# Moving three norms, an hT copy and the row copies of batches 2 and 3 to ScalarE, with new step lists

## What is computed

```python
x = _layernorm(x + _L0_attn_ref(x, ...))     # 16 query heads, 4 kv heads, width 8, RMS norm, rotation,
                                             # softmax(50 tanh(s / 50)), causal
x = _layernorm(x + _L0_xattn_ref(x, ctx...)) # attention to 32 context rows, FiLM, an S4D convolution over
                                             # the sequence (in the Fourier basis), layernorm h, gelu MLP 128-512-128,
                                             # layernorm
x = _layernorm(x + _L0_ffn_ref(x, ...))      # 2 shared experts for all tokens, 8 routed ones, the top 2 per token
```

## Time and profile before

| | |
|---|---|
| runs | 546.08, 549.91, 554.17 us, median 549.91 |
| profiled execution | 546.51 us, span 544.3 us |
| PE busy | 438.0 us, 80% |
| DVE, ACT busy | 332.0 us (61%), 324.6 us (60%) |
| POOL busy | 229.3 us, 42% |
| PE clock granted, mean | 0.926 of full speed |

### The profile page before, as it was taken

One profiled execution on the slowest core, in us unless ns is written; L12 is line 12 of the kernel. 1 busy time (PEld: TensorE's weight loads), 2 busy tenths in 40 slices (PEclk: granted clock), 3 DMA queues, 4 the chain that ended last, 5 costly groups with the idle time before them and its releaser, 6 DMA issues. The chain is left out here.

```text
span 544.3 us, 9650 instructions
## 1 busy us (share of the span) xinstructions
PE 438.0 (80%) x3369; PEld 316.0 (58%) x3369; DVE 332.0 (61%) x991; ACT 324.6 (60%) x541; POOL 229.3 (42%) x296
## 2 busy tenths in 40 slices
PE   3572575577989979978889899899998799898990
PEld 2430141154747834556645677488588797698970
DVE  7989997587575576877662678266266320434224
ACT  4158987758985687967799424413355454364531
POOL 3064616523622064451522441746145677144521
PEclk9996756678989989999999999999998999999996
DMA  3798300004020000000000205203227797779831
GB/s 94 253 219 147 100 2 0 0 1 138 1 81 1 20 0 2 1 0 1 2 1 1 49 31 187 86 11 85 58 83 222 210 314 246 203 234 284 274 98 39
DMA packets 39699, 51.40 MB, mean 94 GB/s; under 512 B 8802, under 2 KB 28804, under 8 KB 39652
## 3 DMA queue, kind: packets, MB, share of 16 engines
q1 hardware_dynamic: 37156, 45.65, 29.3%
q0 software_dynamic: 2496, 5.15, 2.6%
HBM read 41.12 MB, written 13.86 MB: 101 GB/s over the span
## 5 line engine op out<-in xcount | busy, mean ns | idle before, releaser
L1107 ACT ACTIVATE probs<-ring_s 128x512 f32<-128x512 f32 x160 | 84.8, 607 | 30.1 <-PE ring_s L784 21.2
L1299 POOL TENSOR_SCALAR_AFFINE_SELECT probs<-probs 128x256 f32<-128x256 f32 (+1 forms) x96 | 50.4, 557 | 103.3 <-ACT probs L1113 103.2
L1160 ACT ACTIVATE g_ring<-ring_s,w_blk 128x128 f32<-128x128 f32 x184 | 52.5, 370 | 48.8 <-PE ring_s L982 48.7
L784 PE MATMUL ring_s<-qT,kT 128*128 128x512 bf16 (+3 forms) x256 | 60.6, 336 | 24.3 <-ACT probs L1107 20.0
L1113 ACT ACTIVATE probs<-probs 128x2560 f32<-128x2560 f32 x32 | 74.6, 2344 | 1.9
L1221 POOL TENSOR_TENSOR rstd<-var_eps,neg_half 128x4 f32<-128x4 f32 x24 | 24.7, 1027 | 102.0 <-DVE var_eps L1547 101.9
L1350 POOL DMA_INDIRECT token_pairs<-y_blk,x_blk x46 | 44.5, 967 | 34.4 <-DVE y_blk L1893 26.0
L801 PE MATMUL bank_o<-probs,vv 128*32 128x128 f32 (+3 forms) x512 | 46.8, 515 | 9.7 <-POOL probs L1299 9.0
L784 PEld LDWEIGHTS ring_s<-qT,kT 128*128 128x128 bf16 x256 | 21.7, 104 | 55.5 <-ACT probs L1107 41.9
L982 PE MATMUL ring_s<-xT_blk,w_blk 128*128 128x128 f32 x368 | 50.3, 281 | 1.7 <-DMA w_blk<-expert_pack 0.9
L982 PEld LDWEIGHTS ring_s<-xT_blk,w_blk 128*128 128x128 f32 x368 | 45.6, 195 | 3.2 <-ACT g_ring L1160 1.5
(11 more groups left out here) (376 smaller groups left out, 942.3 us busy)
## 6 DMA issues: line engine op xcount, KB each, us to landing
w_blk<-expert_pack SPq DMA_DIRECT2D x46, 514.0 KB, 4.8
expert_pack<-in_L_ffn_W SPq DMA_DIRECT2D x16, 256.0 KB, 9.4
expert_rows<-blank SPq DMA_DIRECT2D x6, 520.0 KB, 3.9
x_blk<-expert_rows SPq DMA_DIRECT2D x10, 260.0 KB, 4.6
y_pair<-token_pairs SPq DMA_DIRECT2D x8, 256.0 KB, 4.0
x_in<-in_x SPq DMA_DIRECT2D x4, 256.0 KB, 3.1
cosm<-in_c_cos SPq DMA_DIRECT2D x1, 1024.0 KB, 7.4
sin_fwd<-in_c_sin_fwd SPq DMA_DIRECT2D x1, 1024.0 KB, 10.4
```

What stands on the lines that cost most here:

```text
L784: last = mm(bank[:, c:c + w], kT[:, r, p // 2, P * j:P * (j + 1)], qT[:, p, P * j:SEQ], start=True, stop=True)
L1107: f(probs[:, pair % PAIRS_HELD, SEQ * n:SEQ * (n + 1)], ring_s[k % BANKS][:, :], ACT.Tanh, scale=1.0 / (CAP * float(np.sqrt(np.float32(HD) ...
L1160: last = f(g_ring[:, s % RING, P * n:P * (n + 1)], ring_s[s % 2][:, P * n:P * (n + 1)], ACT.Gelu, bias=w_blk[:, k % SLOTS, HID + n:HID + n ...
L1299: last = g.affine_select(out=v, in_=v, compare_op=ALU.is_ge, fill=0.0, base=0, pattern=[[0, v.shape[1]], [1, P]], channel_multiplier=-1)
```

## The change

For batches 2 and 3 (`LATER = 2`), DVE no longer scales the tiles in `h`, `ff_norm` and `x2`. It copies rstd and computes -mean * rstd into a small tile `late_scale` (two instructions on 128x4), and ACT applies them with four Identity activations. ACT also takes `hT.2`, `hT.3` and `copies.2`, `copies.3`. All four step lists are written anew, from their start, not only where these steps stand.

```diff
+LATER = 2
+            def norm_late(b, n, src, dst):
+                act.wait_ge(late_scaled[b - LATER], n + 1)
+                for j in range(NT):
+                    last = f(dst[:, j, :], src[:, j, :], ACT.Identity, scale=late_scale[:, b - LATER, n, 0, j:j + 1],
+                             bias=late_scale[:, b - LATER, n, 1, j:j + 1])
+                return last
+
+            def h_step(b):
+                norm_late(b, 0, xt, fa).then_inc(h_ready, 1)
+
+            def ff_norm(b):
+                norm_late(b, 1, xt, fa).then_inc(ff_scaled, 1)
+
+            def x2_step(b):
+                norm_late(b, 2, fa, x2[:, b, :].rearrange("p (j d) -> p j d", j=NT)).then_inc(x2_ready, 1)
+
+            def hT_step(b):
+                act.wait_ge(hT_ps, b + 1)
+                act.wait_ge(up_ps, HC * b)
+                f(hT[:, :], bank_r[:, :], ACT.Copy).then_inc(hT_sb, 1)
+
+            def copy_rows(b):
+                act.wait_ge(x2_ready, b + 1)
+                act.wait_ge(rows_copied, b)
+                if b % GB == 0:
+                    act.wait_ge(scattered[b // GB - 1], 16 * 2 * NT * GB)
+                for k in range(2):
+                    last = f(x_rows[:, k, NT * (b % GB):NT * (b % GB + 1), 0:D], x2[:, b, :].rearrange("p (j d) -> p j d", j=NT), ACT.Copy)
+                last.then_inc(rows_copied, 1)
...
-                if b >= GB and b % GB == 0:
-                    pool.wait_ge(scattered[b // GB - 1], 16 * 2 * NT * GB)
...
+            def norm_later(b, n):
+                roots[0] += 1
+                dve.wait_ge(rstd_ready, roots[0])
+                scale = late_scale[:, b - LATER, n, :, :]
+                op(v.tensor_copy(scale[:, 0, :], rstd[:, :]))
+                stt(out=scale[:, 1, :], in0=mean_var[:, :, 0], scalar=-1.0, in1=rstd[:, :], op0=ALU.mult, op1=ALU.mult).then_inc(late_scaled[b - LATER], 1)
+                dve.wait_ge(late_scaled[b - LATER], n + 1)
...
             def h_step(b):
+                if b >= LATER:
+                    return norm_later(b, 0)
                 norm_end(xt, fa).then_inc(h_ready, 1)
```

(`ff_norm` and `x2_step` on DVE get the same two lines.) Of the lists, one line of DVE's and two of ACT's:

```diff
-    steps squares.0 rms.0 rope.0 parts.0 v.0 copies.0 states qT.0.1 qT.0.3 vf.0 vf.1 vf.2 qT.0.5 pack angles.0
+    steps squares.0 rms.0 rope.0 parts.0 v.0 copies.0 states qT.0.1 squares.1 qT.0.3 vf.0 vf.1 rms.1 vectors pack
...
-    ff_out.1 s.3.7.0 s.3.7.1 s.3.7.2 s.3.7.3 s.3.7.4 exp.3.7 x2T.1 gates_exp.1 blk_gelu.0 blk_gelu.1 blk_gelu.2
-    blk_gelu.3 x1T.3 blk_gelu.4 blk_gelu.5 blk_gelu.6 blk_gelu.7 cross_exp.3 attnT.3 blk_gelu.8 gelu.2.0 gelu.2.1
+    exp.3.6 s.3.7.0 s.3.7.1 s.3.7.2 s.3.7.3 s.3.7.4 exp.3.7 x2T.1 gates_exp.1 blk_gelu.0 blk_gelu.1 x1T.3 blk_gelu.2
+    blk_gelu.3 blk_gelu.4 cross_exp.3 blk_gelu.5 blk_gelu.6 h.2 attnT.3 blk_gelu.7 hT.2 gelu.2.0 gelu.2.1 gelu.2.2
```

More of the change, by code:

```diff
@@ L107 @@
[L107 to L111, removed]
@@ new lines @@
+    mask.3.0 root mask.3.1 shift.1 shape_out.1 resid.1 mask.3.2 root root mask.3.3 mask.3.4 mask.3.5 shift.2 copies.0
+    root ff_norm.1 mask.3.6 root mask.3.7 copies.1 root root shape_out.2 resid.2 root scatter.1.0 scatter.1.1
+    scatter.1.2 scatter.1.3 root ff_norm.2 root scatter.1.4 scatter.1.5 scatter.1.6 shift.3 scatter.1.7 shape_out.3
+    resid.3 root root ff_norm.3 root blk_out.16 blk_out.17 blk_out.18 blk_out.19 blk_out.20 blk_out.21 blk_out.22
+    scatter.3.0 scatter.3.1 scatter.3.2 blk_out.23 blk_out.24 blk_out.25 scatter.3.3 blk_out.26 blk_out.27 blk_out.28
@@ L201 @@
-    turns.0 vectors vf.3 products.0 amounts.0 angles.1 turns.1 angles.2 turns.2 oT.0 products.1 amounts.1 tokens.0
-    squares.1 rms.1 angles.3 turns.3 products.2 w1 oT.1 tokens.1 parts.1 oT.2 tokens.2 amounts.2 copies.1 evacuate.0
-    oT.3 tokens.3 evacuate.1 products.3 yT.0 amounts.3 evacuate.2 qT.1.1 v.1 proj.0 evacuate.3 qT.1.3 qT.1.5 x1.0
-    x_norm.0 xn.0 first_tap squares.2 rms.2 oT.4 cross.0 tokens.4 soften.0 spectra oT.5 parts.2 tokens.5 film.0.0
-    film.0.1 film.0.2 film.0.3 modulate.0 oT.6 copies.2 tokens.6 spectrum.0 v.2 oT.7 qT.2.1 qT.2.3 tokens.7 yT.1
@@ L221 @@
-    weigh.63 weigh.64 blkT.68 blkT.69 weigh.65 blkT.70 weigh.66 blkT.71 weigh.67 weigh.68 weigh.69 weigh.70 weigh.71
-    pairs.2 pairs.3 out_begin.2 settle.77 out_end.2 out_begin.3 out_end.3
+    steps squares.0 rms.0 rope.0 parts.0 v.0 copies.0 states qT.0.1 squares.1 qT.0.3 vf.0 vf.1 rms.1 vectors pack
+    angles.0 turns.0 vf.2 vf.3 qT.0.5 products.0 amounts.0 angles.1 turns.1 oT.0 angles.2 turns.2 products.1 tokens.0
+    amounts.1 oT.1 evacuate.0 angles.3 turns.3 products.2 evacuate.1 tokens.1 oT.2 tokens.2 parts.1 copies.1
@@ new lines @@
+    amounts.2 oT.3 w1 tokens.3 evacuate.2 qT.1.1 yT.0 products.3 amounts.3 qT.1.3 proj.0 evacuate.3 qT.1.5 x1.0 v.1
+    first_tap x_norm.0 squares.2 rms.2 oT.4 cross.0 tokens.4 spectra soften.0 oT.5 film.0.0 tokens.5 film.0.1
+    film.0.2 film.0.3 xn.0 modulate.0 parts.2 copies.2 oT.6 tokens.6 qT.2.1 spectrum.0 oT.7 v.2 qT.2.3 tokens.7 yT.1
+    proj.1 x1.1 shape_out.0 cross.1 h_norm.0 soften.1 h.0 squares.3 hT.0 rms.3 x_norm.1 qT.2.5 oT.8 film.1.0 film.1.1
+    tokens.8 film.1.2 film.1.3 xn.1 modulate.1 oT.9 parts.3 tokens.9 ffT.0 ff_norm.0 oT.10 copies.3 tokens.10
@@ L487, in build @@
         out_scaled = sem("out_scaled")
+        late_scaled = [sem(f"late_scaled{n}") for n in range(B - LATER)]
         pair_used = sem("pair_used")
```

181 lines of the change are left out of this document (93 added, 88 removed).

## The result

The changed kernel takes 530.19 us as the median of four runs (528.00, 530.16, 530.22 and one of 1090.26 that nothing here explains and that the comparison leaves out), beside 551.26 us of the kernel before on the same chip. The ratio is 0.961, 95% interval 0.952 to 0.971. It is faster by 3.9%, twice the 2% or so that I had forecast, and 1.2 us inside the low end of the range of 529 to 551. The profiled executions are closer to each other, 546.51 and 530.16 us, spans 544.3 and 528.3, since the one of before is quicker than all but one of its other runs.

The account below looks back on a forecast made before the run. Bound: early, no engine full, each waiting for others in order; from 163 us PE nearly full. Profiled 546.5, front -7, back -2: 537.5, plus about half of that execution's 3.4 us below the median: 539 us; range 529 to 551.

Parts of the forecast that it names:

- The front's times: Up to batch 1's first tanh: ACT's new list laid out with old durations, that tanh at 116 to 118 against 127.80 us.
- 66.1: Front, ACT's list: from 56.8 us, six tanhs, an exp and the sines of round 1 end at 66.1 us.
- 93: Front, ACT's list: after 81.9 us, ten tanhs and two exps end at 93 us.
- The term for the front: Attention 10 to 12 us earlier, S4D kernel 7; the shorter taken as reaching the end: -7 us, bounds 0 and -12.
- Behind it PE is nearly full and shifts as a whole: After the front: PE's later work moves earlier with the front's lead, no term of its own.
- Rival 3: More goes right: front gains 12 us, back 4, some of PE's 16 idle us from 163 to 299 go: 528; chance 0.13.
- The back: Where the moved steps stand: PE's small waits filled by half units, -2 us, bounds 0 and -4.
- The five gaps: Back: PE's waits of 0.69 to 0.88 us for one copy, 3.8 us in all, filled by half units.
- The floor: First expert group's rows land at about 381.7, PE takes them at 382.80: of 3.0 us only 1.1 usable.
- the half units: Back: shared expert work ahead of each use hides the moved norms, costing PE nothing; otherwise six times 0.8 us.
- Rival 1: The front's lead is not carried: front 0 to -3, back -1, 543 to 548, take 546; chance 0.24.
- Rival 2: Back: ACT stops at six norms for `late_scale`, gelus queue; 2.5 us each, 15 us, gives 554; chance 0.17.

Follow-up runs that it names:

- e_front_old: Changed kernel with the old order ahead of batch 1's first scores: 539.9 us, 9.6 more than the changed kernel rerun beside it, ratio to the kernel before 0.987.
- e_mid_only: Kernel before with the new order only from batch 1's first scores to the first shared expert unit, old engines: 554.66 us, ratio 0.979.
- e_lists_tail: Changed kernel with DVE's old order from `blkT.49`, and norms, hT and row copies back on DVE and POOL: 522.9 us, ratio to the kernel before 0.956.
- e_tail_old: Changed kernel with DVE's old order from `blkT.49` on: 526.23 us, 4.1 less than the changed kernel rerun beside it.
- f_act_pe: Kernel before with the new order of the front on ACT and PE alone: 580.33 us, ratio 1.025.
- f_dve_pool: Kernel before with the new order of the front on DVE and POOL alone: 580.36 us, ratio 1.027.
- e_lists_only: Kernel before with all four new lists, but norms, hT and row copies left on DVE and POOL: 541.3 us, ratio 0.955.
- sets 2 and 4: Two calls of follow-up runs, each on one chip with the kernel before beside them, which took 565.65 and 565.57 us.
- e_norms_back: Changed kernel with DVE's old order from `blkT.49` and the six norms back on DVE, hT and row copies on ACT: 539.03 us, ratio to the kernel before 0.952.
- sets 1 and 3: The call that measured the change and a later call of follow-up runs; the kernel before took 551.26 and 548.17 us in them.
- set 3: One call of follow-up runs on one chip, variants of the changed kernel and its rerun, beside the kernel before at 548.17 us.
- e_changed_again: The changed kernel itself, run once more: 530.33 us beside 548.17 of the kernel before, ratio 0.970.

## Why the prediction was right, and where it was not

The measured time is in the range, by 1.2 us, and that is luck: two terms that the sum does not have, -7.1 us in the middle and +5.4 at the end, nearly cancel. Without the second the time would have been some 525 us, under the range.

- **The front's times were right.** First value product 54.9 us (forecast 51 to 55), idle ahead of pair 7's tanhs 3.27 (under 5), cast 0.41 (near 0.5), last powers of round 3 end at 112.7 (112), first tanh of batch 1 at 117.46 (116 to 118). Laying the new list out by hand with the old durations worked here. Two of its sums are off: "66.1" adds up to 67.4, which the next line has right again, and "93" to 91.6, and these 1.4 us are carried to the end, where they brought the forecast closer to what was measured. The first product came 6.7 us earlier, not 8.
- **The term for the front was too small, -7 for -10.3.** I took the S4D strand, 7 us earlier, as the shorter chain. Wrong as put: the new middle takes 167.6 to 169.5 us behind new and old fronts, whether the strand's last powers end 5 us ahead of batch 1's tanh (changed) or some 7 (e_front_old), so it follows attention, and the strand has slack. The pass has the move of `xT.2` in its 116 to 118, but no price for it; it is worth 2.6 to 4 of the 10.3 us.
- **The middle was the step that failed most.** "Behind it PE is nearly full and shifts as a whole" put a new list over 175 us at zero, and left the idle time there to Rival 3. It gave 7.1 us; e_mid_only shows 5.7 of it alone, behind the old front. In the earlier trace rows PE idles 16 us of 136, and the two rows of its waits shown above would have told that 10 us of the middle hang on two kinds of steps, both of which the new lists move.
- **The back was forecast -2 and gave -3.9** up to the second expert group, as a sum of two things. The order was worth more, 5 to 7 us: e_lists_tail's back is 163.6 us against 168.8, and the moved work costs 3.3 of it by the medians. The five gaps of the earlier trace rows closed. The floor was misread, and the wait of 1 to 2 us at `blkT.16` did not appear. In the trace before, the first load of x_blk, issued at 377.0, landed at 379.9 (the 4.6 us that I used are a median over such loads), so there were 2.9 us of slack and not 1.1. And the scatters did not stay: the first begins at 321.3 instead of 340.9, the sixteenth at 353.4 instead of 374.7. PE takes `blkT.16` at 360.1 without waiting, 22.7 us earlier, of which 17.5 are the last exp's; the back's own lead there is 5.2 us, and 1.3 of it are lost behind.
- **The moved work costs, where I had nothing.** I hid it behind the half units. The cover is there for batch 2: ACT waited 2.83 and 5.05 us for `late_scale` at 336 and 343, against "not over 1 us", and PE lost 0.31. For batch 3 it is not: PE's waits of 0.63, 0.57 and 1.22 us shown above come with the moved work.
- **The end, +5.4 us, was not in any case of mine**: DVE's list was rewritten there too, and I read the change only to the last moved step. By the medians of e_tail_old 4.1 us of it are DVE's order; the rest is not assigned.
- **Rival 1** (lead not carried) is wrong: it is carried whole. **Rival 2** has the right sign for the moved work, 3 to 6 us instead of 15, and ACT does stop as it says, but in the changed kernel the two long stops cost PE 0.31 us, and PE loses more where ACT hardly stops. **Rival 3** is nearest by its time, 528, though its back did not come; the changed kernel got there with 7 us from the middle and 5 given back at the end.

From the -9 of my sum to the -16 of the profiled executions it is thus -3.3 (front), -7.1 (middle), -1.9 (back) and +5.4 (end).

## What to carry to other kernels

A change that is named for moved work and brings new lists is to be read as two changes; here the order, with the old end, gave 4.4% and the moved work took 0.6 back. Cut the span at instructions that both programs have, and give each stage a term of its own, the ones that the description doesn't name and the last one too. In lists that wait for each other, half of a new order can cost more than the whole gives, and a step that nobody needs soon (`out_end.1`, `copies.3`, `xT.2`) is expensive when it waits or works ahead of one that somebody does.

## What the runs showed of the hardware

- **DVE copies beside POOL.** Three copies of 128x1024 bf16 took 3.53 us with POOL's exponents running (before, f_act_pe, e_mid_only) and 1.60 to 1.61 with POOL at its masks instead (changed, f_dve_pool). The 1.92 us between them are about the 1.96 of POOL's first instruction of that step. Batch 0's three, with POOL idle, took 0.95 (before and changed, at 22.2 us). The Trainium skill says in "SBUF — State Buffer", section "Who interferes with whom", that the two engines share a port pair as an exclusive lock; these rows agree. The forecast that the new start would pay 3.4 us for it did not come out: DVE's two `pt` instructions beside POOL's exponents took 2.28 and 1.96 us, before 1.01 and 1.30, so 1.9 us in all; POOL's first exponent took 2.82 us there, before 1.91.
- **The clock.** The granted clock in the front was higher after the change (0.74 for 0.67), and it fell to 0.57 for 4 us behind a wait of 2.3 us. PE's score matmuls took 314 ns in the mean, before 336: 256 of them make 5.6 us of busy time. It is not what made the front shorter: e_lists_only, with the same front, got 0.68 from 38.0 us to its first tanh of batch 1, and that tanh came at 118.2 us, 0.8 later than in the changed kernel.
- **A stall in two sets.** In all kernels of sets 2 and 4 PE stands once for 4.5 to 9.1 us between 405 and 456 us, here in e_norms_back:

```profile
415.95 0.44 PE L659 MATMUL ring_s<-ident,x_blk 128*128 128x128 f32 x1 [9.07 <-issue]
```

The profile shows no releaser. It is not in sets 1 and 3, where neither the old nor the new order shows it; that it belongs to the chip is likely, but no experiment's kernel was traced on both kinds. What it is stays open. It makes up between a third and nine tenths of what the backs are longer by; more idle time and a lower granted clock around it (0.94 to 0.96 in these backs, 0.98 to 1.00 in the others) make up the rest. So a ratio from sets 2 and 4 is not free of it either, and the comparison that carries the argument is that of set 3, e_lists_tail against e_tail_old and e_changed_again.
